# A feed-forward, attention, feed-forward block on one core: the first two expert slots ahead of the last groups, and moved loads, projections and a table load in the attention

## The chip, the cores and the metric

One core of one Trainium2 chip runs the whole program in one launch. The metric is the device time in microseconds (us). The arithmetic is float32: each product of two matrices is made of three matmuls of fp32r operands (the high parts, and twice a high part with a low part), so every operand is held as a pair hi, lo.

## The reference, cut to what matters

x has 2 sequences of 2,048 tokens of 256 channels, 4,096 tokens in all. The same feed-forward block, with the same weights, stands before and behind the attention.

```python
x = x + 0.5 * ffn(layernorm(x))
x = x + attn(layernorm(x))            # causal, one head, Q, K and V of 128 channels
x = x + 0.5 * ffn(layernorm(x))

def ffn(x):
    xln = ln(x, ln1_w, ln1_b)
    x = x + sigmoid(xln @ Wr) * (xln @ Wv) @ Wo
    state = xln @ Ws
    h = ln(x, ln2_w, ln2_b)
    bids = sigmoid(h @ conf) * shares * sigmoid(h @ w_diff) + h @ W_aff    # three bids a token
    w = argmax(bids)                                                       # one expert a token
    out = [square(relu(h @ K[0])) @ V[0],                # K 256 x 1024, V 1024 x 256
           square(relu(h @ K[1])) @ V[1],
           (h @ W1 * sigmoid(state @ W2)) @ W3]
    return x + out[w] * scale(w)
```

## The kernel before

The two feed-forward blocks (FFN1, FFN2) run the same code; FFN1 also loads and splits the weights. Each has two parts.

**Part a, the groups.** 8 groups (NG) of 512 tokens, four tiles of 128 each. For a group: layer norm, transposes, the six products of U(g) (gate, value and state), Wo(g), the second layer norm, T2(g) (transposes of h), bids(g), W1(g), bidT(g), prefix(g) (running counts of the tokens that chose an expert), W3(g). Several groups are in work at once: ffn_a_tensor, ffn_a_scalar, ffn_a_vector and ffn_a_gpsimd each write out their engine's order by hand. On DVE gates(g) and rank(g) work out where each token's row goes, with small instructions of four columns, win_second(g) finishes the gate and w3(g) writes the third expert's part into out_rows. POOL scatters each token's row (h, residual, gate) by indirect DMA into routed_rows in DRAM: tokens of expert 0 from the bottom up, tokens of expert 1 from the top down. The last two groups go in halves (scatter_half, L874), half 0 the normalised row (z), half 1 residual and gate.

**Part b, the slots.** routed_rows is read back in 17 slots (NSLOT), 256 rows each, the last 128. For slot j: the rows are loaded (z_in, L1190, and row_in, L1195, which loads residual and gate), sT(j) transposes them, ACT writes the hi half (shi) and DVE the lo half (slo, L1403 to L1407), K(j) is 48 matmuls in four quarters, ACT makes relu, DVE its square (sq, L1417), ACT the hi half and POOL the lo half of it (hrlo, L1477), V(j) is 48 matmuls, DVE makes the output rows (orow), POOL sends them to their tokens' places by indirect DMA (send). TensorE's order is K(j), sT(j+1), V(j-1). A slot holds tokens of one expert; which one, and which rows, is worked out on DVE after rank of the last group (the slot table, L1149 to L1161), and both the loads and the choice of K or V wait for it (semaphore flag).

**The hand-over** from part a to part b is written out at the end of the ffn_a functions (from `last = NG - 1`) and at the start of the ffn_b functions (slots, first, body). In FFN1 k_bias(e), 32 matmuls of one column with the raw weights K[e], stands there too, and late_sync (L357) loads the raw weights of K, of V and of the attention, which ACT and DVE split into halves (split_hi, split_lo, L388 to L402).

**The attention** has 16 steps (NB), each a block of 256 queries; BLOCKS gives the order. It starts with the first sequence's 8 projections (T, QK, V of a block k), and in steps 0 to 8 the second sequence's projections are made beside the scores. A step s does output(s-2), the two rows of scores of step s (maxima on DVE, exp on ACT), the transposes and the weighing of step s-1. DVE makes the statistics of attn_x, POOL scales it (L2069), both for the projections. PSUM banks are handed out by a fixed rotation that follows the order list of bank_uses. After step 15, ACT normalises group 0 of FFN2 into z_rows (normalize, L644 to L652), and a one-row sigmoid (L1913) has its activation table loaded for FFN2.

TensorE's end of part a:

```python
    W3(last - 1, range(2, GT))
    if s:
        k_bias(pe, b, s, 0)
        k_bias(pe, b, s, 1)
    W3(last)
```

## Time and profile before

| what | us |
|---|---|
| time of the kernel, median of 3 runs | 1061.05 |
| lowest and highest of them | 1060.47, 1067.13 |
| time of the profiled execution | 1064.8 |
| span of the profiled execution | 1063.0 |

In the span FFN1's last slot ends at about 417 us, the attention's first matmuls are at 427 and its last output at about 670. The page of the profile has the busy time of each engine (PE is TensorE's matmuls, PEld its weight loads, DVE VectorE, ACT ScalarE, POOL GpSimd). The windows view has, for each stretch of the span, the busy time of each engine in the order PE, PEld, DVE, ACT, POOL, with the number of instructions in brackets, then the clock that TensorE was granted (1.00 is full), the busy share of the DMA engines and the GB/s. A row of a timeline has the start, the length, the engine, the line, the operation, the tiles written and read, the shapes, how many alike follow each other, and in square brackets the idle time ahead of it with what ended it. The chain of waits is the work that ended last, followed back from the end of the span.

### The profile page before, as it was taken

To read this page: it belongs to the slowest core of one execution; us is meant where nothing else is said; L and a number is where in the kernel's file an instruction comes from. 1 tells how busy PE (TensorE), PEld (TensorE's weight loads), DVE (VectorE), ACT (ScalarE), POOL (GpSimd) and SP (SyncE) were. 2 spreads that over 40 slices of the span, in tenths; PEclk is the share of its full clock that TensorE was granted. 3 is DMA by queue.
4 is the path that set the end of the run, shared out by engine and by line. 5 is a ranking of instruction groups with operands and counts; after the bars stand their busy time and mean duration, and the time that the engine had idled before them with its cause. 6 is when DMAs were issued, how large, how long until landed. Compare 5 with 4: busy or idle time off the path is not lost.

```text
span 1063.0 us, 21617 instructions
## 1 busy us (share of the span) xinstructions
PE 988.0 (93%) x7024; PEld 912.5 (86%) x7025; DVE 688.6 (65%) x1762; ACT 560.1 (53%) x1185; POOL 488.4 (46%) x539
## 2 busy tenths in 40 slices
PE   8999998989999999889987998999999699999997
PEld 7788887989999998878886887778888599999997
DVE  5788877856555552656765667688887764555552
ACT  4767556354445551455543655676665255544452
POOL 3254544376556663821221001225634666666564
PEclk9999998799999999999999999999999799999999
DMA  8521243222122212201232134303112222212220
GB/s 291 198 80 61 100 139 138 82 71 63 59 58 79 68 46 73 75 11 51 84 106 87 53 120 157 102 21 119 61 41 78 77 77 82 61 59 59 59 69 32
DMA packets 51237, 88.96 MB, mean 84 GB/s; under 512 B 5806, under 2 KB 43568, under 8 KB 49968
## 3 DMA queue, kind: packets, MB, share of 16 engines
q1 hardware_dynamic: 42608, 62.60, 19.0%
q0 software_dynamic: 8544, 25.24, 6.2%
q8 instruction: 51, 0.84, 0.3%
q14 instruction: 34, 0.28, 0.1%
HBM read 58.39 MB, written 47.06 MB: 99 GB/s over the span
## 4 chain that ended last, share of the span: by engine, by line
PE 64%; DVE 17%; ACT 6%; issue 5%; DMA 5%; POOL 4%; SPq 0%; DVEq 0%; POOLq 0%; ACTq 0%
PE banks4to L411 30%; PE bank L411 24%; PE banks4to L1715 3%; DVE out_rows L1057 2%; DMA attn_x<-x_after_ffn 2%; DVE pT_lo L1976 2%; DVE gT_lo L959 1%; PE bank L507 1%; DMA routed_rows<-out_rows,row_index 1%; PE bank L1258 1%; DVE zT_lo L948 1%; POOL attn_x L2069 1%; PE bank L1727 1%; PE bank L497 1%; DVE chunk_max L1966 1%
## 5 line engine op out<-in xcount | busy, mean ns | idle before, releaser
L1417 DVE TENSOR_TENSOR relu_squared<-relu 128x512 f32<-128x512 f32 (+1 forms) x136 | 151.0, 1124 | 108.3 <-ACT relu L1366 50.2
L1477 POOL TENSOR_TENSOR hr_lo<-relu_squared,hr_hi 128x512 fp32r<-128x512 f32 (+1 forms) x136 | 182.9, 1357 | 58.7 <-DVE relu_squared L1417 55.5
L1366 ACT ACTIVATE relu<-bank,slot_k_bias 128x256 f32<-128x256 f32 (+1 forms) x204 | 83.5, 460 | 176.6 <-PE bank L411 159.8
L411 PE MATMUL banks4to<-v_hi,hr_hi 128*128 128x256 f32 x528 | 151.8, 288 | 2.5 <-DVE slot_out L1426 2.5
L411 PE MATMUL banks4to<-v_hi,hr_lo 128*128 128x256 f32 x528 | 149.0, 282 | 0.0
L411 PE MATMUL banks4to<-v_lo,hr_hi 128*128 128x256 f32 x528 | 149.0, 282 | 0.0
L411 PE MATMUL bank<-shT_hi,k_hi 128*128 128x256 f32 (+1 forms) x408 | 117.5, 288 | 11.3 <-DVE shT_lo L1407 5.8
L411 PE MATMUL bank<-shT_hi,k_lo 128*128 128x256 f32 (+1 forms) x408 | 115.3, 283 | 0.0
L411 PE MATMUL bank<-shT_lo,k_hi 128*128 128x256 f32 (+1 forms) x408 | 115.2, 282 | 0.0
L411 PEld LDWEIGHTS banks4to<-v_hi,hr_hi 128*128 128x128 f32 x528 | 99.7, 189 | 2.9 <-issue 2.9
L884 POOL DMA_INDIRECT routed_rows<-out_rows,row_index x48 | 48.0, 999 | 116.9 <-DVE row_index L1040 105.9
L411 PEld LDWEIGHTS banks4to<-v_hi,hr_lo 128*128 128x128 f32 x528 | 99.8, 189 | 0.0
L411 PEld LDWEIGHTS banks4to<-v_lo,hr_hi 128*128 128x128 f32 x528 | 99.7, 189 | 0.0
L1374 ACT ACTIVATE hr_hi<-relu 128x512 fp32r<-128x512 f32 (+1 forms) x136 | 84.4, 620 | 15.9 <-ACT relu L1366 6.9
L411 PEld LDWEIGHTS bank<-shT_hi,k_hi 128*128 128x128 f32 x408 | 77.6, 190 | 14.9 <-issue 14.6
L411 PEld LDWEIGHTS bank<-shT_hi,k_lo 128*128 128x128 f32 x408 | 77.7, 190 | 0.0
L411 PEld LDWEIGHTS bank<-shT_lo,k_hi 128*128 128x128 f32 x408 | 77.6, 190 | 0.0
L1861 ACT CAST pT_hi<-bank 128x512 fp32r<-128x512 f32 (+1 forms) x72 | 39.1, 564 | 56.0 <-PE bank L1727 55.7
L1852 ACT ACTIVATE p<-banks4to,minus_row_max 128x512 f32<-128x512 f32 (+2 forms) x80 | 49.8, 628 | 28.8 <-DVE minus_row_max L1969 18.0
L1976 DVE TENSOR_TENSOR pT_lo<-bank,pT_hi 128x512 fp32r<-128x512 f32 (+1 forms) x72 | 46.2, 659 | 22.4 <-ACT pT_hi L1861 21.8
L1484 POOL DMA_INDIRECT x_after_ffn<-slot_out,token_index x33 | 34.6, 1049 | 52.9 <-DVE slot_out L1426 45.5
L1484 POOL DMA_INDIRECT out_x<-slot_out,token_index x33 | 32.8, 995 | 54.0 <-DVE slot_out L1426 45.0
(282 smaller groups left out, 3002.4 us busy)
## 6 DMA issues: line engine op xcount, KB each, us to landing
routed_rows<-in_pad SPq DMA_DIRECT2D x32, 514.0 KB, 5.2
slot_row<-routed_rows SPq DMA_DIRECT2D x32, 258.0 KB
slot_z<-routed_rows SPq DMA_DIRECT2D x32, 256.0 KB
attn_x<-x_after_ffn SPq DMA_DIRECT2D x16, 256.0 KB, 2.9
attn_out<-x_after_ffn SPq DMA_DIRECT2D x16, 256.0 KB, 2.6
x_after_attention<-attn_out SPq DMA_DIRECT2D x16, 256.0 KB, 2.1
x_rows<-x_after_attention SPq DMA_DIRECT2D x8, 512.0 KB, 4.7
x_rows<-in_x SPq DMA_DIRECT2D x7, 512.0 KB, 4.0
```

Source lines behind the costliest of these rows:

```text
L411: mm = pe.matmul(outv, w(pw), m(pm), start=(n_first and k == 0), stop=(n_last and k == 2))
L884: pool.indirect_dma_start(routed, bass.IndirectOffsetOnAxis(b.posi[g % 2][:, t:t + 1].bitcast(U32), 0), b.rows[g % 2][:, t, :], None).then ...
L1057: last = dve.scalar_tensor_tensor(rows[:, t, RES], b.bank(6 + t // 2)[:, (t % 2) * C:(t % 2 + 1) * C], b.gt[p][:, t:t + 1], rows[:, t, RES ...
L1366: last = act.activation(b.r[q % 2][:, h % 2, 0:width(j)], b.bank(1 + q)[:, (h % 2) * SLOT:(h % 2) * SLOT + width(j)], ACT.Relu, bias=b.kbs ...
L1374: act.activation(b.hr[p][0][:, 2 * q:2 * q + 2, 0:width(j)], b.r[q % 2][:, :, 0:width(j)], ACT.Square).then_inc(f["hrhi"], 1)
L1417: dve.tensor_tensor(b.sq[q % 2][:, :, 0:width(j)], r, r, ALU.mult).then_inc(f["sq"], 1)
L1477: pool.tensor_tensor(b.hr[p][1][:, 2 * q:2 * q + 2, 0:n], b.sq[q % 2][:, :, 0:n], b.hr[p][0][:, 2 * q:2 * q + 2, 0:n].bitcast(F32), ALU.su ...
L1484: pool.indirect_dma_start(dst, bass.IndirectOffsetOnAxis(b.idx[p][:, t:t + 1].bitcast(U32), 0), b.o[p][:, t, :], None, bounds_check=N - 1, ...
L1715: mm = pe.matmul(out[:, at:at + n], b.kq[pw][:, q, 0, t * P:(t + 1) * P], part, start=(k == 0 and i == 0 and not last), stop=(k == 2), ski ...
L1852: act.activation(b.p[s % 2][t][:, c * KEYS:c * KEYS + w], bank(("S", s, t, c))[:, 0:w], ACT.Exp, bias=b.nbias[:, s % 2, t:t + 1], accum_ou ...
L1861: act.copy(b.pT[m % 2][0][:, 0:w], b.bank(m % 2)[:, 0:w]).then_inc(a["pthi"], 1)
L1976: dve.tensor_tensor(b.pT[m % 2][1][:, 0:w], b.bank(m % 2)[:, 0:w], b.pT[m % 2][0][:, 0:w].bitcast(F32), ALU.subtract).then_inc(a["ptlo"], 1)
```

## The change

What it does:

- prefix of group 5 also sums the tokens of expert 1. first_slots() on DVE, after rank of group 5, takes slots 0 and 1 from the expert that had the fuller half of groups 0 to 5 (at 1,536 or more of 3,072 tokens: expert 1). Their z rows are loaded when the scatters of groups 0 to 5 have landed.
- Their transposes stand in part a, after bidT of group 7; shi after conf of group 7, slo ahead of g2 of group 7. TensorE's order then is K(0), K(1), W3 of group 7, sT(2), V(0).
- The slot table (now slot_table(), of the slots from 2 on) comes after the lo half of g2T; then sq(0, 0), win_second and w3 of group 6. last_rows (group 7) moves into body(1), behind slo(2).
- On POOL the second halves of group 6 come after hrlo of slot 0, those of group 7 after hrlo of slot 1; before, in FFN1 the former stood ahead of hrlo of slot 0 and the latter behind it, in FFN2 both ahead of it.
- In FFN1, V's weights come as one load of 2 MB when group 4 is asked for (into the place of v_lo), and are split in iterations 3 to 6; the attention's weights are loaded with group 6 and split in slots 1 and 2; K's loads move into ffn_b_sync.
- In the attention V is projected by channel: six matmuls of 256 columns, a copy on ACT (v_turned), two transposes (turn_v), then the halves. In the first phase its two halves lag by one block. The last V, of block 15, is made ahead of the second row of scores of step 8. attn_x is loaded one step further ahead. Group 0 of FFN2 is normalised in step 14 instead of 15, and the sigmoid of L1913 comes in step 16.

The diff, cut to its core:

```diff
@@ -129,26 +132,26 @@
...
-        b.raw_k = [at(f"raw_k{e}", w, [CC, HID]) for e, w in enumerate((2560, 0))]
-        b.raw_v = [at(f"raw_v{e}", w, [HC, C]) for e, w in enumerate((24320, 6656))]
-        b.raw_a = at("raw_attention", 9728, [3 * CC * DK + C])
...
+        b.raw_k = [at(f"raw_k{e}", w, [CC, HID]) for e, w in enumerate((2560, 6656))]
+        b.raw_a = at("raw_attention", 23056, [3 * CC * DK + C])
...
@@ -354,21 +364,6 @@
...
-def late_sync(sp, b, s, f, k_w, v_w, w_qkv):
-    flat = "p a n -> p (a n)"
-    sp.wait_ge(f["T1"], 2 * NG)
-    sp.dma_start(b.raw_a[:], w_qkv).then_inc(s.a, 16)
-    sp.wait_ge(f["U"], 6 * (NG - 1))
-    sp.dma_start(b.raw_k[0][:].rearrange(flat), k_w[:, 0]).then_inc(s.k, 16)
-    sp.wait_ge(f["res"], NG - 2)
-    sp.dma_start(b.raw_k[1][:].rearrange(flat), k_w[:, 1]).then_inc(s.k, 16)
-    sp.wait_ge(f["U"], 6 * NG)
-    sp.wait_ge(f["scat"][(NG - 3) % 2], 16 * GT * (NG - 2) // 2)
-    sp.dma_start(b.raw_v[1][:].rearrange(flat), v_w[:, 1]).then_inc(s.v, 16)
-    sp.wait_ge(f["Wo"], 2 * NG)
-    sp.dma_start(b.raw_v[0][:].rearrange(flat), v_w[:, 0]).then_inc(s.v, 16)
...
         sp.wait_ge(f["res"], g - X_BUFS + 1)
         sp.dma_start(b.x[g % X_BUFS][:], xg[g]).then_inc(f["x_in"][g % X_BUFS], 16)
         if s and g == X_BUFS:
+            sp.dma_start(b.raw_v[:].rearrange("p e a n -> p e (a n)"), v_w).then_inc(s.v, 16)
             for j in range(FILL, NSLOT):
                 fill(sp, f, pad, routed, j)
+        if s and g == X_BUFS + 2:
+            sp.dma_start(b.raw_a[:], w_qkv).then_inc(s.a, 16)
...
@@ -531,9 +530,11 @@
...
+        if g == NG - 1:
+            pe.wait_ge(f["early"], 1)
...
-        if g == NG - 1:
+        if g in (NG - 3, NG - 1):
             mm = pe.matmul(b.bank(5)[:, 2 * GT:2 * GT + 1], b.tri[:, 1], b.e16[:, 2 * GT:2 * GT + 1], start=True, stop=True)
         mm.then_inc(f["pref"], 1)
...
@@ -631,14 +632,17 @@
     bids(last)
     W1(last, 0, 1)
     bidT(last)
+    slot_in(0, 0, 1)
+    slot_in(1, 1, 1)
     W1(last, 1, 2)
     W3(last - 1, range(0, 2))
     prefix(last)
     W3(last - 1, range(2, GT))
     if s:
+        pe.wait_ge(f["slo"], 2)
         k_bias(pe, b, s, 0)
         k_bias(pe, b, s, 1)
-    W3(last)
+    return lambda: W3(last)
...
@@ -794,6 +799,9 @@
...
+        if s and k >= V_FROM:
+            act.wait_ge(s.v, 16)
+            split_hi(act, v_plan(b), k - V_FROM, k - V_FROM + 1, s.v_hi)
...
@@ -805,22 +813,19 @@
...
-        act.wait_ge(s.k, 32)
+        act.wait_ge(s.k0, 16)
         split_hi(act, late, 0, 2, s.k_hi)
     bd(last)
     if s:
+        act.wait_ge(s.k1, 16)
         split_hi(act, late, 2, 3, s.k_hi)
     conf(last)
+    shi(0, 0)
+    shi(1, 1)
     if s:
         split_hi(act, late, 3, K_ITEMS, s.k_hi)
-        act.wait_ge(s.v, 32)
-        split_hi(act, late, K_ITEMS, K_ITEMS + 2, s.k_hi)
     g2_hi(last, 0)
     g2_hi(last, 1)
-    if s:
-        split_hi(act, late, K_ITEMS + 2, KV_ITEMS, s.k_hi)
-        act.wait_ge(s.a, 16)
-        split_hi(act, late, KV_ITEMS, LATE, s.k_hi)
...
@@ -904,8 +909,7 @@
...
-    scatter_half(last - 1, 1)
-    return lambda: scatter_half(last, 1)
+    return lambda g: scatter_half(g, 1)
...
@@ -1042,6 +1047,35 @@
...
+    def first_slots():
...
+        link(dve.tensor_scalar(d, b.bank(5)[:, 2 * GT:2 * GT + 1], float(GROUP * (NG - 2) // 2), None, ALU.is_ge))
...
+        link(dve.scalar_tensor_tensor(b.start[:, two], b.slot_row[:, 2, two], d, b.slot_row[:, 3, two], ALU.mult, ALU.add))
...
+        dve.tensor_copy(b.flagi[:, two], b.flag[:, two]).then_inc(f["early"], 1)
+        dve.wait_ge(f["early"], 1)
...
+    def slot_table():
+        pairs, alone = slice(2, PAIRS), slice(PAIRS, NSLOT)
+        link(dve.tensor_copy(b.n1[:], b.bank(5)[:, 2 * GT:2 * GT + 1]))
...
+        dve.memset(b.cnt[:], 0.0).then_inc(f["flag"], 1)
...
@@ -1128,8 +1162,11 @@
...
+        if s and k >= V_FROM:
+            split_lo(dve, v_plan(b), k - V_FROM, k - V_FROM + 1, s.v_hi, s.v_lo)
     last = NG - 1
     rank(last - 2)
+    first_slots()
...
@@ -1142,45 +1179,43 @@
...
+    if not s:
+        slot.kbs(0, 0)
+        slot.kbs(1, 1)
     bid_sum(last)
     gates(last)
     win_first(last)
     rank(last)
-    link(dve.tensor_copy(b.n1[:], b.bank(5)[:, 2 * GT:2 * GT + 1]))
-    pairs, alone = slice(0, PAIRS), slice(PAIRS, NSLOT)
...
-    win_second(last - 1)
-    w3(last - 1)
+    slot.lo(0, 0)
+    slot.lo(1, 1)
+    g2(last, 0)
+    g2(last, 1)
     if s:
         split_lo(dve, late, 0, K_ITEMS, s.k_hi, s.k_lo)
-    g2(last, 0)
-    g2(last, 1)
     for fc in range(CC):
         dve.wait_ge(f["g2hi"], 2 * last + 1 + fc)
         dve.tensor_tensor(b.g2T[1][:, fc], b.sg[last % 2][:, fc], b.g2T[0][:, fc].bitcast(F32), ALU.subtract
                           ).then_inc(f["g2lo"], 1)
     if s:
-        split_lo(dve, late, K_ITEMS, KV_ITEMS, s.k_hi, s.k_lo)
+        dve.wait_ge(s.kb_mm, 2)
+        dve.tensor_copy(b.kbias[:], b.bank(2)[:, 0:2 * HC].rearrange("p (e h) -> p e h", e=2)).then_inc(s.kb, 1)
+        dve.wait_ge(s.kb, 1)
+        slot.kbs(0, 0)
+        slot.kbs(1, 1)
+    slot_table()
+    slot.sq(0, 0)
+    win_second(last - 1)
+    w3(last - 1)
     dve.wait_ge(f["flag"], 1)
     def last_rows():
...
@@ -1197,17 +1232,28 @@
...
-    sp.wait_ge(f["flag"], 1)
+    if s:
+        sp.wait_ge(f["U"], 6 * (NG - 1))
+        sp.dma_start(b.raw_k[0][:].rearrange("p a n -> p (a n)"), k_w[:, 0]).then_inc(s.k0, 16)
+    sp.wait_ge(f["early"], 1)
     first = [rows_of(j, ST, slice(0, C)) for j in range(2)]
     for p in range(2):
-        sp.wait_ge(f["scat"][p], 16 * GT * NG // 2)
+        sp.wait_ge(f["scat"][p], 16 * GT * (NG - 2) // 2)
     for j in range(2):
         sp.dma_start(b.sz[j][:], first[j]).then_inc(f["s_in"][j], 16)
+    if s:
+        sp.wait_ge(f["U"], 6 * NG)
+        sp.dma_start(b.raw_k[1][:].rearrange("p a n -> p (a n)"), k_w[:, 1]).then_inc(s.k1, 16)
+    first = [rows_of(j, ST, slice(C, ROW)) for j in range(2)]
+    sp.wait_ge(f["res"], NG)
+    for j in range(2):
+        sp.dma_start(b.srow[j][:, :, 0:ROW - C], first[j]).then_inc(f["r_in"][j], 16)
+    sp.wait_ge(f["flag"], 1)
+    for p in range(2):
+        sp.wait_ge(f["scat"][p], 16 * GT * NG // 2)
     for j in range(2, 4):
         z_in(j, j % 2)
     sp.wait_ge(f["late"], 16 * GT * 2)
-    for j in range(2):
-        row_in(j, j)
     with sp.Fori(0, (NSLOT - 5) // 2) as it:
         for par in range(2):
             row_in(it * 2 + 2 + par, par)
@@ -1259,13 +1312,23 @@
...
             hold(pe, f["relu"], j * 4 - 3 + q, cr)
-            if isinstance(j, int) and j == 0 and q == 3:
-                pe.wait_ge(f["slo"], 2)
-            if s and isinstance(j, int) and j == 0 and q == 1:
-                pe.wait_ge(s.kb, 1)
+            if isinstance(j, int) and j == 0:
+                if q == 1:
+                    pe.wait_ge(f["slo"], 2)
+                    if s:
+                        pe.wait_ge(s.kb, 1)
+                if q >= 2:
+                    pe.wait_ge(f["g2"], 2 * NG - 3 + q)
...
@@ -1301,14 +1364,14 @@
...
-    def first():
-        sT(0, 0, 1)
-        sT(1, 1, 1)
-        Kj(0, 0, expert(0))
     def body(j, p, last):
         before, this = expert(j - 1), expert(j)
         Kj(j, p, this)
+        if isinstance(j, int) and j == 1:
+            last_W3()
+            pe.wait_ge(f["flag"], 1)
+            if s:
+                pe.wait_ge(s.v_lo, V_ITEMS)
         if not last:
             sT(j + 1, 1 - p, (j + 1) // 2 + 1 if isinstance(j, int) else loads_of(j, p))
@@ -1318,12 +1381,10 @@
         return half[0] + (1 if p else 0)
     half = [None]
-    pe.wait_ge(f["flag"], 1)
+    pe.wait_ge(f["early"], 1)
     if s:
         pe.wait_ge(s.k_lo, K_ITEMS)
-    first()
-    if s:
-        pe.wait_ge(s.k_lo, KV_ITEMS)
+    Kj(0, 0, expert(0))
     for j in (1, 2):
         body(j, j % 2, False)
...
@@ -1375,20 +1443,24 @@
...
-        shi(0, 0)
-        shi(1, 1)
         relu(0, 0)
     def body(j, p, last):
         relu(j, p)
         if not last:
             shi(j + 1, 1 - p)
+        if s and isinstance(j, int) and j == 1:
+            act.wait_ge(s.a, 16)
+            split_hi(act, late_plan(b), K_ITEMS, LATE, s.k_hi)
...
@@ -1428,31 +1508,20 @@
...
             kbs(j + 1, 1 - p)
         sq(j, p)
         if not last:
             slo(j + 1, 1 - p)
+        if isinstance(j, int) and j == 1:
+            last_rows()
         orow(j - 1, 1 - p, uses)
...
-        split_lo(dve, late_plan(b), KV_ITEMS, LATE, s.k_hi, s.k_lo)
+        split_lo(dve, late_plan(b), K_ITEMS, LATE, s.k_hi, s.k_lo)
     n0 = n[0]
...
@@ -1487,13 +1556,14 @@
...
+        if isinstance(j, int) and j == 1:
+            last_halves(NG - 1)
         pool.drain()
         send(j - 1, 1 - p)
     def first():
         hrlo(0, 0)
-        if last_halves:
-            last_halves()
+        last_halves(NG - 2)
...
@@ -1622,7 +1698,7 @@
...
-        while ahead < 2 * QB and ahead <= QB + s + 2:
+        while ahead < 2 * QB and ahead <= QB + s + 3:
...
@@ -1688,12 +1764,18 @@
...
-        out = b.bank(k - QB + 4) if k in LATE_V else bank(("V", k))
...
+        for c in range(CC):
+            mm = passes(pe, out[:, 0:SLOT], lambda p: b.Wvv[:, c, p * DK:(p + 1) * DK], lambda p: z_of(k)[p][:, c],
+                        c == 0, c == CC - 1)
+        mm.then_inc(a["V"], 1)
...
+    def turn_v(k):
+        pe.wait_ge(a["vt"], k + 1)
...
+            mm = pe.transpose(v_bank(b, k)[:, SLOT + t * DK:SLOT + (t + 1) * DK], b.vt[:, 2 * to + t], b.ident[:])
+        mm.then_inc(a["VN"], 1)
...
@@ -1792,18 +1879,26 @@
         if ks:
             project_qk(ks[0])
         weigh_some(s - 1, min(1, half), half)
+        if s == QB:
+            project_v(LAST_V)
         if s < NB:
             for c in range(chunks_of(s)):
                 scores(s, 1, c)
+                if s == QB and c == 0:
+                    turn_v(LAST_V)
+        if s == 0:
+            for k in LATE_V:
+                turn_v(k)
         weigh_some(s - 1, half, min(half + 2, n))
         if ks:
             project_v(ks[0])
         for k in ks[1:]:
             zT(k)
         weigh_some(s - 1, min(half + 2, n), n)
+        if ks:
+            turn_v(ks[0])
         for k in ks[1:]:
             project_qk(k)
-            project_v(k)
...
@@ -1832,13 +1927,17 @@
...
-    def v_hi(k):
+    def v_turned(k):
         to = value_slot(k)
         act.wait_ge(a["V"], k + 1)
         if k > QB:
             act.wait_ge(a["PV"], pairs_before(k - QB))
-        out = b.bank(k - QB + 4) if k in LATE_V else bank(("V", k))
-        act.copy(b.v[0][:, 2 * to:2 * to + 2], out[:, 0:SLOT].rearrange("p (t n) -> p t n", t=ST)
+        act.copy(b.vt[:, 2 * to:2 * to + 2], v_bank(b, k)[:, 0:SLOT].rearrange("p (t n) -> p t n", t=ST)).then_inc(a["vt"], 1)
+    def v_hi(k):
+        to = value_slot(k)
+        act.wait_ge(a["VN"], k + 1)
+        act.copy(b.v[0][:, 2 * to:2 * to + 2], v_bank(b, k)[:, SLOT:2 * SLOT].rearrange("p (t n) -> p t n", t=ST)
                  ).then_inc(a["vhi"], 1)
...
@@ -1903,15 +2007,17 @@
...
-                v_hi(ks[0])
+                v_turned(ks[0])
                 for k in ks[1:]:
                     z_hi(k)
+        for k in LATE_V if s == 0 else ks[:1]:
+            v_hi(k)
         for k in ks[1:]:
             qk_hi(k)
-            v_hi(k)
-        if s == NB - 1:
+        if s == NB - 2:
+            normalize(act, b, f, 0, range(GT))
+        if s == NB:
             act.activation(b.cmax[:, 0, 0:ST], b.half[:, 0, 0:ST], ACT.Sigmoid)
-            normalize(act, b, f, 0, range(GT))
...
@@ -2030,19 +2132,20 @@
...
+        if s == QB:
+            v_lo(LAST_V)
         for c in range(chunks):
             maxima(s, 1, c)
         for j in range(turned, min(turned + 2, n)):
             pair(s - 1, j)
-        if ks:
-            v_lo(ks[0])
         for k in ks[1:]:
             z_lo(k)
         for j in range(turned + 2, n):
             pair(s - 1, j)
+        for k in LATE_V if s == 0 else ks[:1]:
+            v_lo(k)
         for k in ks[1:]:
             qk_lo(k)
-            v_lo(k)
         for k in ks:
...
```

## Rows read from the trace of the kernel before

**Rows 1.** Page, part 1: busy us (share of the span) xinstructions of each engine.

```profile
PE 988.0 (93%) x7024; PEld 912.5 (86%) x7025; DVE 688.6 (65%) x1762; ACT 560.1 (53%) x1185; POOL 488.4 (46%) x539
```

**Rows 2.** Windows: stretch, us, each engine's busy us (count), granted clock, DMA share, GB/s.

```profile
101.70:122.20 20.50, 20.17 (x124) 17.56 (x123) 17.66 (x63) 13.72 (x27) 10.79 (x16) 1.00 0.22 79
228.40:234.50 6.10, 6.06 (x38) 6.07 (x39) 3.38 (x7) 2.85 (x6) 3.26 (x4) 0.72 0.44 123
434.00:456.00 22.00, 19.92 (x167) 19.10 (x165) 16.11 (x43) 10.27 (x20) 19.71 (x25) 1.00 0.25 74
655.00:661.70 6.70, 5.29 (x41) 4.42 (x39) 5.29 (x18) 3.60 (x10) 2.61 (x6) 1.00 0.72 235
840.40:847.20 6.80, 0.03 (x1) 0.00 (x0) 6.44 (x23) 1.24 (x2) 4.97 (x6) 0.68 0.27 97
847.20:852.50 5.30, 5.28 (x24) 5.28 (x25) 1.92 (x9) 0.00 (x0) 2.13 (x3) 0.50 0.59 175
```

**Rows 3.** Timeline of TensorE: start us, us, what, [wait before it, and releaser].

```profile
188.26 11.24 PE L375 MATMUL bank<-ln_cols,raw_k 128*128 128x1 f32 x64
...
228.44 0.57 PE L411 MATMUL bank<-shT_hi,k_hi 128*128 128x256 f32 x1 [3.55 <-DVE shT_lo L1407]
...
884.77 0.36 PE L411 MATMUL bank<-shT_hi,k_hi 128*128 128x256 f32 x1 [0.23 <-issue]
```

**Rows 4.** Timeline of DVE and TensorE in step 6 of the attention.

```profile
560.41 0.75 DVE L1934 BATCH_NORM_STATS2 bn_parts<-attn_x 128x6 f32<-128x256 f32 x2 [1.81 <-DMA attn_x<-x_after_ffn]
...
561.81 0.39 PE L411 MATMUL bank<-wao_hi,oT_hi 128*128 128x256 f32 x1 [2.44 <-DVE oT_lo L1981]
```

**Rows 5.** Timeline of ACT and TensorE, end of the attention.

```profile
661.02 1.28 ACT L1913 ACT_TABLE_LOAD   x1
...
662.43 2.06 ACT L652 ACTIVATE z_rows<-x_rows,rsqrt_work 128x256 f32<-128x256 f32 x4
...
665.25 0.52 PE L411 MATMUL bank<-wao_hi,oT_hi 128*128 128x256 f32 x1 [3.58 <-DVE oT_lo L1981]
```

**Rows 6.** Chain of waits: start us, us, what (FFN1's slots, attention).

```profile
242.40 4.50 PE bank L411 x36
...
494.67 1.44 PE banks4to L411 x12
...
504.03 1.31 PE banks4to L411 x12
```

**Rows 7.** Timeline of DVE, hand-overs of FFN1 and FFN2 (last row).

```profile
199.77 4.62 DVE L402 SCALAR_TENSOR_TENSOR v_lo<-raw_v,v_hi 128x1024 fp32r<-128x1024 f32 x4
...
209.86 1.66 DVE L1057 SCALAR_TENSOR_TENSOR out_rows<-banks4to,trans_gate,out_rows 128x256 f32<-128x256 f32 x4
...
211.44 1.28 DVE L1417 TENSOR_TENSOR relu_squared<-relu 128x512 f32<-128x512 f32 x2
...
213.98 2.31 DVE L1417 TENSOR_TENSOR relu_squared<-relu 128x512 f32<-128x512 f32 x2 [1.26 <-POOL hr_lo L1477]
...
216.21 1.26 DVE L1397 TENSOR_SCALAR slot_k_bias_part<-k_bias,slot_expert 128x8 f32<-128x8 f32 x1
...
227.60 0.68 DVE L1407 TENSOR_TENSOR shT_lo<-bank,shT_hi 128x512 fp32r<-128x512 f32 x1
...
841.21 0.16 DVE L1160 CAST slot_expert_int<-slot_expert 128x17 int32<-128x17 f32 x1
```

**Rows 8.** Timeline of POOL, hand-overs and the attention's first projections (second row).

```profile
212.27 2.87 POOL L1477 TENSOR_TENSOR hr_lo<-relu_squared,hr_hi 128x512 fp32r<-128x512 f32 x2 [13.02 <-DVE relu_squared L1417]
...
441.37 2.44 POOL L2069 TENSOR_SCALAR attn_x<-attn_x,mean_var,rsqrt_work 128x256 f32<-128x256 f32 x2
...
831.57 1.89 POOL L874 DMA_INDIRECT routed_rows<-out_rows,half_row_index  x1 [0.17 <-issue]
...
854.41 0.96 POOL L874 DMA_INDIRECT routed_rows<-out_rows,half_row_index  x1 [4.47 <-DVE out_rows L1057]
...
858.20 0.96 POOL L874 DMA_INDIRECT routed_rows<-out_rows,half_row_index  x1 [0.30 <-issue]
```

## What the change should do to the time

> **What bounds the kernel now.** I read the page first, then the windows, the chain of waits, then the timelines of TensorE, DVE, ACT and POOL at the places the diff touches. TensorE is busy 93% of the span [rows 1], so a change is worth what it takes from TensorE's instruction stream or from its 75 us of idle and slow-clock time. Inside the group loop there is almost nothing to take: 20.17 of 20.50 us are busy, with DVE at 17.66 [rows 2]. What can be taken lies at three kinds of places. The hand-over from the groups to the slots: 6.8 us with one matmul in FFN2, then 5.3 us at half clock [rows 2]; in FFN1 one-column matmuls of 11.24 us, later a wait of 3.55 us [rows 3]. The attention's steps with projections: a wait of 2.44 us [rows 4]. The end of the attention: 3.58 us [rows 5].
>
> I follow "K(j)", "V(j)": the two expert products of slot j, 48 matmuls each. Twelve of 256 columns take 1.44 us [rows 6], so 0.12 each and 5.7 us a product. In the kernel before, K(3) starts at 242.4 in FFN1 and at 884.8 in FFN2 [rows 3, 6], and from there on slots follow every 12 us with TensorE full. The hand-over is therefore worth what K(3) starts earlier.
>
> **The group loop of FFN1.** Four copies of V's halves on ACT and four on DVE now lie in iterations 3 to 6. On DVE four took 4.62 us [rows 7], 1.15 each. DVE has 2.8 us of idle in an iteration [rows 2]; in iterations 3 and 4 the next statistics still follow, and I take 0.4 of each as reaching TensorE: 0.8 lost. If every 1.15 showed, 4.6 would be lost; if none, 0. In return only one MB of K is loaded beside the scatter in iteration 6, 0.4 won by estimate. Term: -0.4. first_slots() is nine small DVE instructions of 0.16 [rows 7], so 1.5 us; it stands ahead of work whose consumer comes 3 us later: nothing.
>
> **The hand-over in FFN2.** DVE used to do the slot table (twelve small instructions of 0.16, 1.9), win_second (eight, 1.3) and w3 of group 6 (1.66) [rows 7] before g2T_lo, whose end at 847.2 released TensorE [rows 2]. Now two slot lo halves (0.68 each [rows 7], 1.36) stand there instead, and TensorE does 8 transposes (0.7) ahead: g2T_lo ends at 847.2 - 4.8 + 1.4 + 0.4 = 844.2, the table (13 small instructions, 2.0) at 846.2. K(0) runs from 841.0 to 846.7, K(1) to 852.4, so TensorE's hole of 6.8 is filled. But then comes a relay between DVE and POOL, written in fixed order. From T, the first square (846.2):
> - four squares with two pairs of hr_lo between: the last square ends at T+4.85 (from 211.44 to 216.29), the last hr_lo at T+7.3 (212.27 + 2.87, then as much again) [rows 7, 8].
> - win_second of group 6: the one small instruction that met hr_lo took 1.26, where others take about 0.16 [rows 7]; so I let two of them wait till T+7.3 and the rest take 1.1: T+8.4. w3 1.66: T+10.1 = 856.3. TensorE has waited 3.9 for it, and does W3(7) partly at half clock.
> - POOL's four late halves of group 6: 854.41 to 859.16 for four [rows 8], with the pitch 1.27, 5.1 with the wake-up 5.3: T+15.4. Only then hr_lo of slot 1: pair 2.87, two squares 1.2, slot_lo 0.7: T+20.1, second pair till T+22.
> - last_rows (win_second again behind hr_lo, then w3): T+24.7. Late halves of group 7: T+29.9. send(0), two more of the same: T+32.4. First hr_lo pair of slot 2: T+35.3, squares T+36.5, slot_lo T+37.2.
> So K(3) can start at 883.4, 1.4 earlier than before. V(1) ends at 878.6 by TensorE's own work (856.3 + 4.3 + 4 x 5.7 - the 0.8 of overlap and transposes), so TensorE idles nearly 5 us and comes back slow: after 3.55 us of idle, 38 matmuls took 6.06 at a granted clock of 0.72 [rows 2, 3], 1.5 over 38 x 0.12. Term: 1.4 - 1.5 = -0.1. Bounds: with POOL never waiting the relay is T+29.5 and the term is +9; if each of the ten DMAs costs 1.89 as the first at 831.57 did [rows 8], it is -9.
>
> The Trainium skill (SBUF — State Buffer, "Who interferes with whom") says that a DVE instruction with two SBUF inputs and a GpSimd instruction that reads SBUF exclude each other, the one that starts first going first. The 1.26 agrees with it. By that rule win_second waits as I have it; without it the relay would be 2.4 shorter in each FFN.
>
> **The hand-over in FFN1.** k_bias (11.24 [rows 3]) ends at 199.5 + 0.8 = 200.3; then k-bias copies and table on DVE, 3.3: T = 203.9. K(0) runs at half clock like the W3 that stood there before (24 in 5.3 at 0.50 in FFN2 [rows 2]), which spreads the squares by 2.2. K(3) at T + 39.4 = 243.3 against 242.4, and slow: -0.9 - 1.8 = -2.7. Bounds: +6.7 (POOL never waits) and -10.
>
> **Attention, start.** POOL sets the pace of the first projections: it is busy 19.71 of 22.0 us with 25 instructions [rows 2], four a block, so 3.5 us a block, of which 2.44 is the scaling of two tiles [rows 8]; TensorE is busy 19.92. V now takes 6 matmuls of 256 columns (0.72) and two transposes (0.18); before, twelve of 128 columns took 1.31 [rows 6], not less per matmul than 256 columns, so 0.4 to 0.5 less work each. While POOL sets the pace this is worth nothing, except in the first round, where T(2) stands behind V(0) at low clock: 1.1. Ahead of the second row of scores the two late V values no longer stand ahead of DVE's maxima: about 2.0, less 0.5 for their copies put later: 1.5. Bounds of both together 0.5 to 3.5.
>
> The Trainium skill (TensorE: Matmul & The Clock Gate, "Back-to-back issue gap") gives about 81 ns for a sustained 128-column matmul; by that V would have cost 1.0 and the edit would save 0.1. The row of 1.31 decides against it here.
>
> **Steps 1 to 8.** Each V goes through an ACT copy, a transposition, a second ACT copy and DVE, and statistics stand behind it. In steps 1 and 2 the 0.5 counts, in 3 and 4 the longer route costs 0.3: +0.4 together. In steps 5 and 6 DVE waited for a load of attn_x (1.81 in step 6 [rows 4], in step 5 I take 1.1) and TensorE for oT_lo behind it (2.44 [rows 4]); loads one step ahead take that off: +3.3. Bound: 2.9, what DVE waited, to 4. Step 7 +0.5. In step 8 V(15) is put before the second row of scores, whose maxima and exp decide when TensorE goes on; it and DVE's v_lo ahead of the maxima add 1.4: -1.4.
>
> **End.** ACT did a table load (1.28 [rows 5]) and four z_rows (2.06) ahead of oT_hi, so TensorE waited 3.58 [rows 5], then ran slow. z_rows now come a step earlier, in a hole of about 2.0 (they delay oT_hi(13) by 1.5), and the load stands behind what TensorE needs: output(14) at 663.1 instead of 665.25, 2.1, and about 0.9 of slow clock: +3.0. Bounds 0.5 and 3.6 + 1.4.
>
> **Sum.** -0.4 - 2.7 + 1.1 + 1.5 + 0.4 + 3.3 + 0.5 - 1.4 + 3.0 - 0.1 = 5.2 us. The profiled execution has a span of 1063.0 and a time of 1064.8; it becomes 1057.8 and 1059.6. The median of the runs is 3.75 lower, 1061.05: 1055.9, I say 1056.
>
> **Rivals.**
> A, the hand-overs pay. If win_second isn't held up and POOL starts each part at once, the relay shrinks towards T+29.5; half way gives about +6 in FFN2 and +3 in FFN1, with 8 from the attention: 17 us, 1044. For it: the small instructions are only four columns wide, and just one row shows such a clash. Against: the late halves are eight DMAs of 1.27 in each FFN, in series with hr_lo whatever DVE does. 0.20.
> B, slower: the indirect DMAs of the relay cost more. 20 of them (four, four and two in each FFN) lie on my path; from 0.26 more for each, the gain of 5.2 is gone. At 1.89 [rows 8] for half of them it is +6 to +9 us over my forecast: 1063 to 1065, for all 1072. For it: they now issue while DVE is squaring. Against: the four of 854.41 [rows 8] cost 0.96 each. 0.15.
> C, the clock falls in the first projections: TensorE would be busy some 2.7 of 3.5 us. At half clock a block takes 4.7, five blocks lose 6: 1062. Against: 79% busy was granted 1.00 [rows 2]. 0.08.
> D, the loads are hidden anyway and DVE stays the limit in steps 3 to 6: 3 less, 1059. 0.12.
> The slots' early rows come in time: their loads can go out when the scatter of group 5 has landed, over 5 us before the transposes.
>
> **Numbers.** My forecast holds 0.45. Within 1% (10.6 us, about what a measurement of this kernel can tell from no change) lie it, C, D and most of B; faster by more than 1%, below 1050.4, is A and a rest of the forecast's own tail; slower is B's end. Range 1045 to 1067, the likeliest case alone 1050 to 1061.
>
> **What would show it.** K(0) starts near 841 and 200.4; TensorE waits nearly 4 us before W3 of group 7 in FFN2 and 4 to 5 us before K(3) in both, with POOL's L874 work in series between hr_lo of slots 0, 1 and 2. DVE never waits for attn_x after the first blocks; output(14) starts 2 us after its predecessor's place. If K(3) starts before 240 and 880 (in the old time scale), my relay is wrong and A holds; if after 246 and 887, B.

## The result

| what | before | changed |
|---|---|---|
| median, us (20 runs each) | 1064.5 | 1067.67 |
| lowest and highest, us | 1060.47, 1067.84 | 1065.25, 1070.07 |
| profiled execution, us | 1064.8 | 1065.25 |
| its span, us | 1063.0 | 1063.3 |

The ratio is 1.0027, 95% interval 1.0016 to 1.0038: 3 us slower, where 5 us faster was forecast. One caution stands ahead of every trace below: the profiled execution of the changed kernel is the fastest of its 20. Its mean granted clock is 0.977; the 20 runs have 0.971 to 0.977, the slower ones on the whole the lower. So the trace shows 0.3 us of the 3.2 between the medians, and single traces of this kernel are good to 2 or 3 us.

First the page of the changed kernel, part 1, to be read beside [rows 1]: TensorE is busy 10.6 us less, and its span is no shorter. It saved work and got holes.

```profile
PE 977.4 (92%) x6962; PEld 902.7 (85%) x6963; DVE 690.1 (65%) x1780; ACT 564.4 (53%) x1201; POOL 488.3 (46%) x539
```

The windows of the changed kernel, columns as in [rows 2]: FFN1's K(3) with the first of sT(4), then FFN2's K(0) and K(1), the wait behind K(1), the wait ahead of K(3), and K(3).

```profile
242.83:251.54 8.71, 8.71 (x50) 8.71 (x51) 4.47 (x13) 4.05 (x9) 5.76 (x5) 0.65 0.33 93
836.90:848.70 11.80, 11.77 (x96) 11.58 (x96) 10.20 (x24) 9.24 (x20) 8.86 (x8) 1.00 0.31 91
848.70:851.84 3.14, 0.01 (x1) 0.03 (x1) 2.96 (x11) 0.39 (x1) 0.38 (x1) 1.00 0.00 0
874.50:882.23 7.73, 0.01 (x1) 0.03 (x1) 3.40 (x5) 0.00 (x0) 6.09 (x6) 0.67 0.35 103
882.23:890.40 8.17, 8.17 (x50) 8.17 (x51) 2.94 (x8) 3.67 (x8) 5.15 (x5) 0.69 0.36 99
```

The hole of 6.8 us that [rows 2] shows ahead of W3 is gone: K(0) and K(1) fill it at full clock. Two others came in its place, 3.1 and 7.7 us, and K(3) then begins slow: 0.65 and 0.69 granted over its stretch, which is the lower of the clock's two levels (1.2 and 2.4 GHz) for most of it. From the first matmul of K(3) to the transposes behind it are 8.6 us in FFN1 and 8.1 in FFN2, where the kernel before has 5.8.

The timeline of TensorE in the changed kernel, columns as in [rows 3], shows who was waited for: W3 of group 7 and K(3) in FFN2, K(3) in FFN1, and in the attention the first weighing of step 3 and output(13).

```profile
242.83 0.55 PE L406 MATMUL bank<-shT_hi,k_hi 128*128 128x256 f32 x1 [8.28 <-DVE shT_lo L1479]
...
513.41 0.39 PE L406 MATMUL bank<-pT_hi,values_hi 128*128 128x256 f32 x1 [1.15 <-DVE pT_lo L2081]
...
661.09 0.39 PE L406 MATMUL bank<-wao_hi,oT_hi 128*128 128x256 f32 x1 [1.63 <-DVE oT_lo L2086]
...
851.84 0.35 PE L406 MATMUL banks4to<-w_hi,g2T_hi 128*128 128x256 f32 x1 [3.13 <-DVE out_rows L1091]
...
882.23 0.55 PE L406 MATMUL bank<-shT_hi,k_hi 128*128 128x256 f32 x1 [7.73 <-DVE shT_lo L1479]
```

The table sets stages of the two traces side by side. The third column is worked out from the timeline of TensorE: how much earlier (+) or later (-) the end of the stage comes in the changed kernel, less the same at its start.

| stage | forecast | traces |
|---|---|---|
| FFN1's groups, to bids(7) | -0.4 | +0.5 |
| hand-over of FFN1, to sT(4) | -2.7 | -3.8 |
| FFN1's slots from 4 on | 0 | -0.9 |
| first projections, to the first scores | +1.1 | +0.6 |
| step 0, to QK of step 1 | +1.5 | +1.4 |
| steps 1 to 4 | +0.4 | -2.1 |
| steps 5 and 6 | +3.3 | +3.1 |
| step 7 | +0.5 | +1.3 |
| step 8 | -1.4 | -2.2 |
| end of the attention | +3.0 | +3.7 |
| FFN2's groups, to bids(7) | 0 | +0.7 |
| hand-over of FFN2, to sT(4) | -0.1 | -2.1 |
| FFN2's slots from 4 on | 0 | -0.6 |
| sum | +5.2 | -0.4 |

### The profile page after: what moved, and what is told of

It reads as the page before. It is cut to its first block, busy times and chain, and to the rows that moved or that the text cites. A ratio compares the mean times of both kernels' runs of the same rounds, so it can differ in the third digit from the quotient of the medians.

```text
span 1063.3 us, 21537 instructions
## 1 busy us (share of the span) xinstructions
PE 977.4 (92%) x6962; PEld 902.7 (85%) x6963; DVE 690.1 (65%) x1780; ACT 564.4 (53%) x1201; POOL 488.3 (46%) x539
## 4 chain that ended last, share of the span: by engine, by line
PE 63%; DVE 20%; issue 6%; ACT 5%; POOL 4%; DMA 1%; POOLq 0%; DVEq 0%; ACTq 0%; SPq 0%
PE banks4to L406 28%; PE bank L406 24%; PE banks4to L1797 3%; DVE out_rows L1091 2%; DVE pT_lo L2081 2%; PE bank L506 2%; DVE gT_lo L964 1%; PE bank L1809 1%; DVE chunk_max L2071 1%; POOL routed_rows L879 1%; DVE zT_lo L953 1%; PE bank L1311 1%; DVE r_gate L958 1%; ACT p L1951 1%; PE bank L370 1%
## 5 line engine op out<-in xcount | busy, mean ns | idle before, releaser
L1489 DVE TENSOR_TENSOR relu_squared<-relu 128x512 f32<-128x512 f32 (+1 forms) x136 | 147.6, 1098 | 122.7 <-POOL hr_lo L1546 56.5
L406 PE MATMUL bank<-shT_hi,k_hi 128*128 128x256 f32 (+1 forms) x408 | 120.3, 295 | 22.2 <-DVE shT_lo L1479 16.8
L406 PE MATMUL bank<-shT_hi,k_lo 128*128 128x256 f32 (+1 forms) x408 | 118.1, 289 | 0.0
L406 PE MATMUL bank<-shT_lo,k_hi 128*128 128x256 f32 (+1 forms) x408 | 117.8, 289 | 0.0
L406 PEld LDWEIGHTS bank<-shT_hi,k_hi 128*128 128x128 f32 x408 | 81.1, 199 | 25.8 <-issue 25.3
L406 PEld LDWEIGHTS bank<-shT_hi,k_lo 128*128 128x128 f32 x408 | 81.3, 199 | 0.0
L406 PEld LDWEIGHTS bank<-shT_lo,k_hi 128*128 128x128 f32 x408 | 81.1, 199 | 0.0
```

Source lines behind the costliest of these rows:

```text
L406: mm = pe.matmul(outv, w(pw), m(pm), start=(n_first and k == 0), stop=(n_last and k == 2))
L1489: dve.tensor_tensor(b.sq[q % 2][:, :, 0:width(j)], r, r, ALU.mult).then_inc(f["sq"], 1)
```

## The experiments

Each kernel was timed in five rounds; all medians stand beside one of the kernel before from the same chip (1063.3 to 1065.8), and the ratio is to that. Differences in us between two experiments are of their medians; where the chips differ, they carry the difference of the chips too, up to 2.5 us.

**Each half of the change alone.** `attn_only` is the kernel before with the diff's hunks from BLOCKS on, `slots_only` the changed kernel without them.

> The kernel before with the attention's part of the change alone (V by channel, attn_x one step further ahead, V(15) ahead of the second row of scores, normalisation in step 14, table load in step 16); the hand-overs to the slots are those of before. Theory 1, from the two traces: between FFN1's slots and FFN2's last group the changed kernel gains 5.6 to 6.5 us, all of it here, so 5 to 7 us faster than before (ratio 0.994), with steps 1 to 4 losing 2 us and step 8 another 2. Theory 2, that of the forecast: 8.4 us faster. Theory 3, the gain is only the luck of the granted clock: within 2 us of before.

> The changed kernel with the attention of before; the early slots, the moved weight loads and splits stay. Theory 1, from the traces: the hand-overs lose 3.7 and 2.2 us, the later slots 1.3, the group loop of FFN1 gains 0.5, so 6 to 9 us slower than before. Theory 2, that of the forecast: 3.2 us slower. Theory 3: the parts hold each other up, and without the attention's part this one is no slower than before.

Measured: `attn_only` 1058.0, ratio 0.9936 (0.9915 to 0.9956), 6.2 us faster. `slots_only` 1072.78, ratio 1.0069 (1.0049 to 1.0088), 8.6 us slower. Theory 1 holds for both. The change is a good half and a bad half; the sum of the two, +2.4, is near the +3.2 measured together. The clock alone (theory 3) is out for `attn_only`. In `slots_only` the clock has a part: the first projections, which have the code of before there, took 2.2 us longer, at a granted clock of 0.55 over their first 10.6 us. The windows are of `slots_only` and of the kernel before:

```profile
429.50:440.10 10.60, 8.91 (x43) 8.68 (x44) 5.01 (x13) 3.71 (x7) 7.14 (x10) 0.55 0.20 53
```

```profile
426.50:437.10 10.60, 8.86 (x63) 8.62 (x64) 6.52 (x18) 4.36 (x10) 7.55 (x12) 0.84 0.25 75
```

**What holds K(3).** Two edits of a few lines to the changed kernel.

```diff
# gates_first, ffn_a_vector
-    slot.sq(0, 0)
     win_second(last - 1)
+    win_second(last)
+    slot.sq(0, 0)
     w3(last - 1)
...
     def last_rows():
-        win_second(last)
         w3(last)
# send_first, ffn_b_gpsimd, body
-        if isinstance(j, int) and j == 1:
-            last_halves(NG - 1)
         pool.drain()
         send(j - 1, 1 - p)
+        if isinstance(j, int) and j == 1:
+            last_halves(NG - 1)
```

> The changed kernel with win_second of groups 6 and 7 both ahead of the squares of slot 0 on DVE, so that their small instructions don't meet hr_lo on POOL. Theory 1, the relay between DVE and POOL sets K(3): in the trace win_second took 3.5 us of T+4.8 to T+8.3 and 2.9 us again for group 7, ahead of the squares it should take 0.9 each, so the relay is 3.5 + 2.9 - 1.8 = 4.6 us shorter in each FFN, K(3) starts near 237.5 and 877.5, and the kernel is 7 to 12 us faster than the changed one (with less slow clock). Theory 2, POOL alone sets the relay: POOL's work is the same, so under 3 us. Theory 3, TensorE loses at K(1) what it wins at K(3), since the first squares start 1.8 later: about nothing.

> The changed kernel with POOL's second halves of group 7 behind the send of slot 0 and not ahead of it; nothing else is moved. Theory 1: POOL stood 3.2 us between the last of the four half scatters and the first of send(0) (871.92 to 875.13), where it otherwise stands 1.0; that is a drain that waits for the scatters just issued. With the drain ahead of them 2.2 to 2.5 us are saved in each FFN, K(3) starts near 879.7, and the kernel is 4 to 5 us faster than the changed one. Theory 2: the 3.2 is the send's own wait (for its rows or semaphores) and moves with it: nothing is saved.

Measured: `gates_first` 1059.84, ratio 0.9947 (0.9927 to 0.9967), 7.8 us under the changed kernel. `send_first` 1063.39, ratio 0.9991 (0.9978 to 1.0005), 4.3 under it. Both are theory 1. In `gates_first` K(3) starts at 240.53 and 879.85, not near 237.5 and 877.5: counted from bids of group 7 that is 3.1 and 2.8 us earlier than in the changed kernel, less than the 4.6 of the relay, and the drain below grew by 0.7. The timeline of DVE, first in the changed kernel, then in `gates_first`, shows the same instruction with hr_lo running on POOL and without:

```profile
846.60 1.25 DVE L1033 TENSOR_TENSOR gate_work<-gate_work 128x4 f32<-128x4 f32 x1
847.89 1.21 DVE L1034 TENSOR_TENSOR gate_work<-gate_work 128x4 f32<-128x4 f32 x1
849.13 0.17 DVE L1035 TENSOR_SCALAR gate_work<-gate_work 128x4 f32<-128x4 f32 x1
```

```profile
842.72 0.15 DVE L1033 TENSOR_TENSOR gate_work<-gate_work 128x4 f32<-128x4 f32 x1
...
843.99 0.15 DVE L1033 TENSOR_TENSOR gate_work<-gate_work 128x4 f32<-128x4 f32 x1
```

1.25 against 0.15 for four columns. In the changed kernel POOL ran two hr_lo from 846.23 to 849.08; L1033 ended at 847.85 and L1034 at 849.10, each as one of them was done. That is the rule of the Trainium skill (SBUF — State Buffer, "Who interferes with whom") that the forecast weighed, and the experiment bears it out: both are instructions with two inputs in SBUF. (The row of 1.26 that the forecast put beside the rule has one tensor as input, k_bias, and one value per partition, so it shows a small instruction held up by hr_lo, but not this case of the rule. The instruction behind it in the trace of the kernel before, L1400 at 217.51, has two and took 1.22.) Then the timeline of POOL, first of the changed kernel, then of `send_first`, at the end of the four half scatters of group 7:

```profile
870.96 0.96 POOL L879 DMA_INDIRECT routed_rows<-out_rows,half_row_index  x1 [0.30 <-issue]
875.13 1.00 POOL L1553 DMA_INDIRECT out_x<-slot_out,token_index  x1 [3.21 <-issue]
876.44 0.99 POOL L1553 DMA_INDIRECT out_x<-slot_out,token_index  x1 [0.30 <-issue]
877.43 2.52 POOL L1546 TENSOR_TENSOR hr_lo<-relu_squared,hr_hi 128x512 fp32r<-128x512 f32 x2
```

```profile
867.59 1.08 POOL L1553 DMA_INDIRECT out_x<-slot_out,token_index  x1 [4.27 <-DVE slot_out L1506]
868.98 0.98 POOL L1553 DMA_INDIRECT out_x<-slot_out,token_index  x1 [0.30 <-issue]
870.26 0.96 POOL L879 DMA_INDIRECT routed_rows<-out_rows,half_row_index  x1 [0.30 <-issue]
...
874.07 0.96 POOL L879 DMA_INDIRECT routed_rows<-out_rows,half_row_index  x1 [0.30 <-issue]
875.06 1.27 POOL L1546 TENSOR_TENSOR hr_lo<-relu_squared,hr_hi 128x512 fp32r<-128x512 f32 x1
```

The 3.21 stands at the line `pool.drain()`; the rows to be sent were ready at 866.95. Between a hr_lo and a send whose rows are ready it costs 1.0 to 1.4 us; behind four indirect DMAs it cost 3.2 to 3.4, in `gates_first` even 3.9. With the drain ahead of them hr_lo of slot 2 starts at 875.06 instead of 877.43.

**Both together, and one step further.** `relay_short` has both edits; `halves_within` moves the late halves of group 7 again, into hrlo of slot 2.

```diff
     def hrlo(j, p):
         for q in range(HC // 2):
+            if isinstance(j, int) and j == 2 and q == 2:
+                last_halves(NG - 1)
```

> The changed kernel with both edits to the relay: win_second of groups 6 and 7 ahead of the squares of slot 0, and the second halves of group 7 behind send(0) on POOL. Apart they gave 7.8 and 4.3 us against the changed kernel's 1067.7. Theory 1, the relay sets K(3) and the two act on different waits of it: they add up, 10 to 12 us, so 1055.5 to 1058, K(3) near 877 in FFN2. Theory 2, they take the same slack (POOL is the bound after the first): no more than the first alone, about 1060.

> relay_short (1055.6 us) with the second halves of group 7 on POOL one place further back, between the second and the third hr_lo of slot 2. Theory 1, K(3) waits for slot 3's lo half, that for the squares of slot 2, and those for POOL, which in relay_short spends 5.0 us on the four half scatters ahead of hr_lo of slot 2: with them behind the second hr_lo the squares go on 5 us earlier, V(1) sets K(3), the waits of 3.4 us ahead of K(3) and the 1.5 of slow clock behind it go in both FFNs: 7 to 10 us faster, 1046 to 1049. Theory 2, the wait only moves to V(2), which needs all four hr_lo of slot 2, then 5 us later: within 2 us of relay_short.

Measured: `relay_short` 1055.63, ratio 0.9917 (0.99 to 0.9934): 12.0 under the changed kernel, the sum of 7.8 and 4.3, so the two act on different waits of one relay. `halves_within` 1053.8, ratio 0.991 (0.9888 to 0.9932): only 1.8 better, where 7 to 10 was expected; the trace is of its slowest run, 1058.91. The timeline of TensorE in `relay_short` (first line) and in `halves_within` says why:

```profile
873.04 0.35 PE L406 MATMUL bank<-shT_hi,k_hi 128*128 128x256 f32 x1 [3.42 <-DVE shT_lo L1479]
```

```profile
872.22 0.36 PE L406 MATMUL bank<-shT_hi,k_hi 128*128 128x256 f32 x1 [0.22 <-issue]
...
881.67 0.45 PE L1311 MATMUL bank<-ident_sb,slot_z 128*128 128x128 f32 x1 [3.47 <-DMA slot_z<-routed_rows]
```

K(3) waits no more, as theory 1 has it, but sT(4) does, for its rows: a third way that neither theory named. In the load queue z of slot 4 stands behind the wait for all late halves, and these now land later. `best` is `halves_within` with V of the second sequence by token (below); `best_z4` is `best` with another order in that queue.

```diff
# best_z4, ffn_b_sync
+    z_in(4, 0)
     sp.wait_ge(f["late"], 16 * GT * 2)
-    with sp.Fori(0, (NSLOT - 5) // 2) as it:
+    row_in(2, 0)
+    z_in(5, 1)
+    row_in(3, 1)
+    with sp.Fori(1, (NSLOT - 5) // 2) as it:
```

> halves_within and V of the second sequence by token together. The edits lie in different stages, so they add up: 2.5 us faster than halves_within, 9 to 12 us (theory 1) or 3 us (theory 2) faster than relay_short's 1055.6.

> best (1052.1 us) with one change of order in the load queue of part b: the z rows of slot 4 are asked for ahead of the wait for the late halves, the residual rows of slot 2 behind it, those of slot 3 after z of slot 5. Theory 1: in best, TensorE waits 4.05 and 3.73 us for slot_z of slot 4, because the queue stands at the late halves (issued until 873.4 in halves_within) before it may ask for it; with z of slot 4 asked for first these waits and about 1 us of slow clock behind each go: 6 to 9 us faster, 1043 to 1046. Theory 2: V(2) waits for the hr_lo behind the halves anyway, so only 2 to 3 us of it come back: 1049 to 1050.

Measured: `best` 1052.07, ratio 0.9896 (0.9875 to 0.9917), 1.7 us under `halves_within`, where 2.5 was expected. `best_z4` 1040.97, ratio 0.9774 (0.975 to 0.9797): 11.1 us (13 by the ratios, for the two are from different chips) from one reordered load, more than the 6 to 9 expected, and 2.3% faster than the kernel before. The timeline of TensorE has first the two waits of `best` ahead of sT(4), in FFN1 and FFN2, then sT(4) and K(4) of `best_z4` in FFN2:

```profile
244.63 0.62 PE L1311 MATMUL bank<-ident_sb,slot_z 128*128 128x128 f32 x3 [4.05 <-DMA slot_z<-routed_rows]
...
874.67 0.45 PE L1311 MATMUL bank<-ident_sb,slot_z 128*128 128x128 f32 x1 [3.73 <-DMA slot_z<-routed_rows]
```

```profile
863.52 0.60 PE L1315 MATMUL bank<-ident_sb,slot_z 128*128 128x128 f32 x4
...
870.66 0.36 PE L406 MATMUL bank<-shT_hi,k_hi 128*128 128x256 f32 x1 [0.79 <-DVE shT_lo L1483]
```

And the windows of FFN2: in `best` from 1 us into K(3) to the end of V(2), with the wait between them, then in `best_z4` from the start of K(3) to the end of V(3):

```profile
866.00:883.44 17.44, 13.60 (x95) 13.26 (x93) 7.35 (x8) 6.13 (x13) 10.97 (x9) 0.80 0.33 93
```

```profile
857.69:882.74 25.05, 24.27 (x201) 23.89 (x200) 15.46 (x20) 12.35 (x26) 18.86 (x16) 1.00 0.30 89
```

Counted from bids of group 7, K(4) starts 5.1 us earlier in FFN1 and 5.7 in FFN2. The waits were 7.8 us in all; the clock behind them (0.80 in the stretch of `best`, 1.00 in that of `best_z4`) makes up most of the rest.

**The attention's edits one by one,** each taken out of `attn_only` (1058.0).

```diff
# loads_as_before, attention_sync
-        while ahead < 2 * QB and ahead <= QB + s + 3:
+        while ahead < 2 * QB and ahead <= QB + s + 2:
# z_rows_late, attention_scalar
-        if s == NB - 2:
+        if s == NB - 1:
             normalize(act, b, f, 0, range(GT))
# v15_as_before: by_token(k) is k == LAST_V; v_second_by_token: it is k >= QB
+        if by_token(k):    # project_v: twelve matmuls of 128 columns, no turn_v
...
-        if s == QB:
-            project_v(LAST_V)
...
         for k in ks[1:]:
             project_qk(k)
+            project_v(k)
```

> attn_only (1058.0 us) with the last V, that of block 15, made as in the kernel before: by token, at the end of step 7, its halves there too; nothing of it stands ahead of the second row of scores of step 8. Theory 1, from the traces: step 8 lost 1.5 us there and 0.7 of slow clock behind it, so 1.5 to 2.5 us faster than attn_only, with the start of step 9 earlier by that. Theory 2: the work has only another place, and step 7 loses what step 8 gains: within 0.7 us of attn_only.

> attn_only with V of all eight blocks of the second sequence made by token as before (twelve matmuls of 128 columns, one hi copy, one lo); by channel stay those of the first sequence. Theory 1: the longer route (a copy, two transposes, a second copy) ends late on DVE, and that is what steps 1 to 4 lose (2.1 us from step 1 to step 5 in the trace, with a wait of 1.0 to 1.2 for the first pT_lo of each step where before it was 0.3 to 0.4): 3.5 to 5 us faster than attn_only, V(15) included. Theory 2: steps 1 to 4 lose it through the loads of attn_x, which now come one step earlier and bring the statistics forward onto DVE: no more than v15_as_before.

> attn_only with the normalisation of FFN2's group 0 on ACT in step 15 as before, the table load still in step 16. Theory 1: the two edits at the end pay for different waits. z_rows in step 14 cost output(13) 1.5 us (wait of 1.63 for oT_lo) and spare output(14) 2.1; so this one is 0.5 to 1.5 us slower than attn_only. Theory 2: all of the gain at the end is the table load, and this one is as fast or faster.

> attn_only (1058.0 us) with the loads of attn_x as far ahead as in the kernel before. Theory 1: the waits of DVE for attn_x in steps 5 and 6 come back (1.1 and 1.8 us), and TensorE's for oT_lo with them: 2.5 to 3.5 us slower than attn_only. Theory 2: the loads are hidden anyway, and the 3.1 us that steps 5 and 6 gain come from V's new way: no slower.

Measured: `v15_as_before` 1057.96, ratio 0.9944 (0.9928 to 0.9961); `v_second_by_token` 1055.42, ratio 0.9916 (0.9898 to 0.9934); `z_rows_late` 1059.89, ratio 0.9954 (0.9939 to 0.9969); `loads_as_before` 1062.92, ratio 0.9995 (0.9979 to 1.001).

V(15) in its old place: the medians show nothing, and the ratio is no better; in the traces step 9 begins 1.1 us earlier, from a start 0.4 later, and output(13) 1.8 earlier. The interval of the ratio is 2 us to either side, so this one is open at that size for the whole kernel. For step 8 the traces settle it: from its first scores to those of step 9 it takes 1.4 to 1.5 us longer than before in each of the eight traces with the early V(15) (changed, `attn_only`, `z_rows_late`, `loads_as_before`, `gates_first`, `send_first`, `relay_short`, `halves_within`), and no longer in the four whose V(15) is made as before (`v15_as_before`, `v_second_by_token`, `best`, `best_z4`). In `v15_as_before` the end of the attention took 1.2 us more than in `attn_only`, but so it did in `relay_short`, which has the early V(15): that is the execution and not the edit. The lines of TensorE, the first scores of step 9, are `attn_only`'s, then `v15_as_before`'s:

```profile
581.62 0.47 PE L1728 MATMUL banks4to<-kq_hi 128*128 128x512 f32 x1 [2.19 <-ACT p L1882]
```

```profile
580.53 0.48 PE L1738 MATMUL banks4to<-kq_hi 128*128 128x512 f32 x1 [1.88 <-ACT p L1896]
```

V by token for the second sequence gave 2.6 us in the medians, less than the 3.5 to 5 expected, and the intervals of the two ratios overlap. In its trace steps 1 to 4 give back 1.7 of their 2.1 and step 8 another 1.4. Theory 2, the loads, is out: `loads_as_before` has the loads of before and loses the same 2.1 in steps 1 to 4. The first weighing of step 3, `attn_only` first, has the wait of the changed kernel, and by token the 0.37 of before:

```profile
508.95 0.39 PE L412 MATMUL bank<-pT_hi,values_hi 128*128 128x256 f32 x1 [1.15 <-DVE pT_lo L2012]
```

```profile
510.14 0.39 PE L412 MATMUL bank<-pT_hi,values_hi 128*128 128x256 f32 x1 [0.37 <-DVE pT_lo L2026]
```

The loads one step ahead are worth 4.9 us by the medians, 4.3 by the traces, more than the 2.5 to 3.5 expected and more than any other edit of the attention. Without them DVE waits and TensorE behind it, as in [rows 4] (these are `loads_as_before`'s, step 6):

```profile
560.92 0.43 DVE L1971 BATCH_NORM_STATS2 bn_parts<-attn_x 128x6 f32<-128x256 f32 x1 [2.46 <-DMA attn_x<-x_after_ffn]
...
562.32 0.39 PE L412 MATMUL bank<-wao_hi,oT_hi 128*128 128x256 f32 x1 [3.11 <-DVE oT_lo L2017]
```

At the end of the attention `attn_only` waits 1.63 for output(13) and no longer for output(14); `z_rows_late` has it the other way round (the second line), 1.9 us slower by the medians, a little over the 0.5 to 1.5 of theory 1. Both edits at the end pay: in the traces the end of the attention is 1.6 us shorter than before with the later table load alone (`z_rows_late`) and 3.7 with both. Each of these is one trace, and the clock decides much of it: of the eleven traces with both edits seven have the 3.7, two have 2.5 (`v15_as_before`, `relay_short`) and two 0.2 (`gates_first`, `halves_within`). In those two the clock fell to the lower level behind the wait of 1.63 ahead of output(13), as the window of `gates_first` from there on shows, which `attn_only` passed at 1.00:

```profile
659.00:666.00 7.00, 6.95 (x32) 6.30 (x32) 3.26 (x11) 2.88 (x6) 0.28 (x2) 0.50 0.52 175
```

```profile
656.56 0.39 PE L412 MATMUL bank<-wao_hi,oT_hi 128*128 128x256 f32 x1 [1.63 <-DVE oT_lo L2017]
```

```profile
662.38 0.58 PE L412 MATMUL bank<-wao_hi,oT_hi 128*128 128x256 f32 x1 [2.07 <-DVE oT_lo L2017]
```

## Why the prediction was wrong

**The relay was read rightly, one term was missing.** The forecast counted from T, the first square. In the changed kernel's FFN2 T is 841.83. The last hr_lo of slot 0 was put at T+7.3 and ends at 849.08, T+7.25. w3 of group 6 was put at T+10.1 and ends at 851.69, T+9.9. The late halves of group 6 were put at T+15.4 and end at 857.35, T+15.5; last_rows at T+24.7 and ends at 866.09, T+24.3; the late halves of group 7 at T+29.9 and end at 871.92, T+30.1. Then "send(0), two more of the same: T+32.4": here the step failed. send(0) ended at 877.43, T+35.6, because the drain in front of it stood 3.2 us behind four indirect DMAs, as `send_first` showed. The diff shows the drain between last_halves and send, and the sum has no term for it. From there all is late: K(3) at T+40.4 instead of T+37.2. In FFN1 the drain stood 3.3 us, and K(3) came at T+40.8 instead of T+39.4, since the squares were spread by 0.4 us and not by 2.2. One line of the working is wrong as written: from W3 of group 7 to the end of V(1) lie three products of 5.7 us and not four. The 878.6 fits three (851.84 to 874.51 was measured, 22.7 us, which from 856.3 gives 879.0); four would have given 882.6 and hardly a hole.

**The clock behind the hole was under-sized.** The forecast took 1.5 us in FFN2 from the stretch behind a wait of 3.55 us [rows 2, 3], and 1.8 in FFN1 without a row. Behind 7.73 and 8.28 us of idle the first 36 matmuls of K(3) took 6.77 and 7.28 us, against 4.50: 2.3 and 2.8. That is 0.8 and 1.0 more than the terms. The length of the hole doesn't explain it: in `slots_only` K(3) of FFN1 lost 1.5 behind a wait of 8.18 us, in `relay_short` 2.5 behind one of 3.91. T itself came earlier than forecast, by 1.4 us in FFN1 and 2.0 in FFN2, both counted from bids of group 7. So FFN1's hand-over is 1.0 worse than forecast (K(3) 1.4 later from a T 1.4 earlier, and the clock), FFN2's 2.0 (3.2 later from a T 2.0 earlier, and 0.8 of clock); the slots from 4 on lost 1.5 that no term had, and FFN1's groups gained 0.9 more. The forecast of 3.2 us lost in the slots' half becomes 3.2 + 1.0 + 2.0 + 1.5 - 0.9 = 6.8 in the traces, and `slots_only` has 8.6 by the medians, with the 2.2 of its first projections in it. The drain cost 3.2 us in each FFN; that the hand-overs came out only 1.1 and 2.0 worse than forecast is luck, the earlier T and in FFN1 the squares that weren't spread.

**The absolute times stood on a low base.** The forecast put the kernel before at 1061.05, the median of three runs; that of 20 is 1064.5. On it the forecast of 5.2 us would read 1059.3, and the measured 1067.67 is still 8.4 above.

**Rival A named the right lever.** It said that the hand-overs would pay if win_second weren't held up; they are held up as the forecast has it. Moving both of them out of the way was worth 7.8 us, with K(3) earlier by 3.1 and 2.8, where the forecast put 2.4 to the hold-up in each FFN. That isn't the hold-up alone: win_second's own 1.3 us, twice, left the relay too and delayed T. Its other reason against, POOL's eight DMAs in series with hr_lo, held too: only `halves_within` with `best_z4`, which take them out of the relay, brought the rest. Rival B (dearer DMAs) was wrong: the halves cost 0.96 to 1.26 each. Its times, 1063 to 1072, were the nearest, for another reason. Rival C didn't come: behind the first 10 us of the first projections the clock stayed at 1.00 to the first scores. Rival D was wrong by `loads_as_before`.

**Steps 1 to 4 had the wrong sign.** The forecast put +0.4, counting 0.5 us less work for steps 1 and 2 and 0.3 of longer route for 3 and 4. The traces have -2.1, 0.4 to 0.7 in every step, and `v_second_by_token` returns 1.7. V's route through two copies and two transposes ends behind the step's last pairs on DVE, and the statistics and the next step's maxima stand behind it; the first pT_lo is 0.8 later in each step. TensorE's saved work was real (QK and V of a block took 2.95 us before, 2.6 with the turn now, 0.35 less: nearly the 0.4 that the forecast took from the row of 1.31 in [rows 6], and not the 0.1 that it worked out from the Trainium skill, TensorE: Matmul & The Clock Gate, "Back-to-back issue gap") and worth nothing where DVE was the limit.

**The rest of the attention was right, in part by luck.** Steps 5 and 6 gave 3.1 for 3.3, but as 3.9 from the loads less 0.8 that V's new way cost there (`loads_as_before` is 0.8 behind the kernel before in these steps), a cost that the forecast didn't have; step 0 1.4 for 1.5, the start 0.6 for 1.1, the end 3.7 for 3.0 (0.2 where the clock fell), step 8 -2.2 for -1.4 (0.7 of it slow clock, which `v_second_by_token` has too, without the early V(15)). `attn_only` was 6.2 us faster than before where the terms sum to 8.4; steps 1 to 4 are the 2.5.

**What stays open.** In the changed kernel the slots from 4 on take 0.6 to 0.9 us more in each FFN, though none of their code was edited; `attn_only` doesn't show it, `relay_short` does. Most of it is in K(j), which takes 5.82 us in a slot where it took 5.77, over 13 slots. The new places of hr, relu_squared and the others in the arena are a suspect, but `best_z4` has them too and its K(j) takes 5.77. The cause stays open. So does what sets the clock's loss behind a wait.

## What to carry to other kernels

Work that fills a hole on one engine is worth what the next wait leaves of it: write the relay out past the hole, with every instruction that issues DMAs and every drain, until the steady state is reached. When a relay is shortened, look at the load queue next: here one load that stood behind an unrelated wait hid 11 us, and it showed only after the relay in front of it had been cut. A shorter instruction stream on the busiest engine gains nothing in a stage where another engine's order releases it.

## What the runs showed of the hardware

- A drain on POOL between a hr_lo and a send whose rows were ready took 1.0 to 1.4 us; behind four indirect DMAs just issued 3.2 to 3.9.
- A DVE instruction of 4 columns with two SBUF inputs took 1.25 us beside a running POOL tensor_tensor and 0.15 without it.
- In the changed kernel TensorE came back after 7.7 to 8.3 us of idle with a granted clock of 0.65 to 0.69 over the next 8 to 9 us, and lost 2.3 to 2.8 us over 36 matmuls. After the 3.1 us ahead of W3 in FFN2 its 24 matmuls took 4.36 us, after 1.2 us in FFN1 2.98.
- The length of a wait did not order its price: the 48 matmuls of K(3) lost 1.5 us behind 3.42 (`relay_short`), 5.52 (`send_first`) and 8.18 (`slots_only`), and 2.8 behind 5.84 (`gates_first`) and 8.28 (changed). Behind the same 1.75 us W3 of FFN2 took 2.98 us in `gates_first` and `best`, 4.59 in `relay_short`. Behind the same 1.63 us ahead of output(13) the granted clock was 1.00 over 7 us in `attn_only` and 0.50 in `gates_first`.
- 20 runs of one kernel spread over 4.8 us, with granted clocks of 0.971 to 0.977, the slower runs on the whole with the lower clock; `best_z4`, with the holes gone, was granted 0.982 to 0.987.
